# Four heads of the rotary self-attention are projected straight into the row tiles of the scores

## What is computed

```python
x = _layernorm(x + _L0_attn_ref(x, ...), axis=-1)
x = _layernorm(x + _L0_xattn_ref(x, ctx_1024, ...), axis=-1)
x = _layernorm(x + _L0_ffn_ref(x, ...), axis=-1)
x = _layernorm(x + _L1_attn_ref(x, L1_attn_Wq, L1_attn_bq, ...), axis=-1)
x = _layernorm(x + _L1_xattn_ref(x, ctx_1024, ...), axis=-1)
x = _layernorm(x + _L1_ffn_ref(x, ...), axis=-1)

def _L1_attn_ref(x, Wq, bq, Wk, bk, Wv, bv, Wo, bo):
    B, S, D, H = (4, 512, 256, 16)
...
    rx = _apply_rope(x)      # [x1 cos - x2 sin, x1 sin + x2 cos] over the two halves of the features

    def proj(W, bias):
        y = rx @ W.T + bias
        return y.reshape(b, s, h, hd).transpose(0, 2, 1, 3)
    q, k, v = (proj(Wq, bq), proj(Wk, bk), proj(Wv, bv))
    scores = jnp.einsum('bhqd,bhkd->bhqk', q, k) / np.sqrt(hd)
    attn = jax.nn.softmax(scores, axis=-1)
    attended = jnp.einsum('bhqk,bhkd->bhqd', attn, v)
    attended = attended.transpose(0, 2, 1, 3).reshape(b, s, d)
    return attended @ Wo.T + bo
```

## Time and profile before

| | us |
|---|---|
| median of 3 runs | 1947.82 |
| lowest and highest run | 1942.93, 1952.94 |
| the profiled execution | 1955.06 |
| its span in the profile | 1953.7 |
| `self_heads`, its first DMA | 560.7 |
| `self_heads`, first and last score matmul of L1566 | 612.8, 977.4 |

### The profile page before, as it was taken

One profiled execution on the slowest core, in us unless ns is written; L12 is line 12 of the kernel. 1 busy time (PEld: TensorE's weight loads), 2 busy tenths in 40 slices (PEclk: granted clock), 3 DMA queues, 4 the chain that ended last, 5 costly groups with the idle time before them and its releaser, 6 DMA issues. The chain is left out here.

```text
span 1953.7 us, 23728 instructions
## 1 busy us (share of the span) xinstructions
PE 1667.5 (85%) x7451; PEld 1216.7 (62%) x7451; DVE 1146.5 (59%) x2249; ACT 1012.8 (52%) x1936; POOL 985.7 (50%) x832
## 2 busy tenths in 40 slices
...
DMA packets 96930, 146.43 MB, mean 75 GB/s; under 512 B 22727, under 2 KB 61836, under 8 KB 93974
## 3 DMA queue, kind: packets, MB, share of 16 engines
...
## 5 line engine op out<-in xcount | busy, mean ns | idle before, releaser
L2414 POOL TENSOR_TENSOR STp_lo_use<-ST_use,STp_hi_use 128x512 fp32r<-128x512 f32 x256 | 338.0, 1330 | 197.2 <-ACT ST_use L2244 195.8
L1890 POOL TENSOR_TENSOR STp_lo<-ST,STp_hi 128x512 fp32r<-128x512 f32 x192 | 248.3, 1313 | 103.6 <-ACT ST L1651 102.3
L2309 DVE TENSOR_REDUCE nmax_use<-bank 128x1 f32<-128x512 f32 x256 | 173.4, 679 | 107.9 <-PE bank L2149 103.4
L2240 ACT ACTIVATE STp_hi_use<-bank 128x512 fp32r<-128x512 f32 x256 | 153.1, 598 | 158.8 <-PE bank L2175 154.8
L1777 DVE TENSOR_REDUCE nmax<-bank 128x1 f32<-128x512 f32 x256 | 170.8, 683 | 51.6 <-PE bank L1566 50.7
L1566 PE MATMUL bank<-rows_k,rows_q 65*128 65x512 f32 x256 | 134.5, 534 | 39.4 <-DVE nmax L1777 21.1
L2244 ACT ACTIVATE ST_use<-bank 128x512 f32<-128x512 f32 x256 | 151.7, 593 | 2.0 <-POOL STp_lo_use L2414 2.0
L1648 ACT ACTIVATE STp_hi<-bank 128x512 fp32r<-128x512 f32 x192 | 116.8, 608 | 57.7 <-PE bank L1577 57.3
L2149 PE MATMUL bank<-ks,qs 128*128 128x512 f32 x256 | 110.6, 433 | 9.4 <-DMA ks<-ks 8.8
L1651 ACT ACTIVATE ST<-bank 128x512 f32<-128x512 f32 x192 | 117.8, 614 | 0.0
...
L2159 PE MATMUL bank<-qs,ks 128*128 128x512 f32 x256 | 103.0, 402 | 7.2 <-DMA q<-rowbuf_use 7.1
...
...
## 6 DMA issues: line engine op xcount, KB each, us to landing
...
rows_q<-hop_scratch SPq DMA_DIRECT2D x32, 256.0 KB, 4.5
...
rows_k<-hop_scratch SPq DMA_DIRECT2D x24, 256.0 KB, 5.6
hop_scratch<-qkp_hi SPq DMA_DIRECT2D x20, 256.0 KB
...
```

The source lines that it names most:

```text
L1890: G.tensor_tensor(parts_of(u)[1], ST[u % TB], plain(parts_of(u)[0]), ALU.subtract).then_inc(low.sem, low.inc(u))
L2240: A.activation(STp[u % NHI][0], bk.ap, ACT.Exp)
L2309: V.tensor_reduce(nmax[:, (h % 2) * TB + j:(h % 2) * TB + j + 1], bk.ap, AX.X, ALU.max, negate=True).then_inc(bk.free, 1)
L2414: G.tensor_tensor(STp[u % NHI][1], ST[u % NFULL], plain(STp[u % NHI][0]), ALU.subtract).then_inc(low["pool"].sem, low["pool"].inc(u))
```

## The change

The first quarter of the first batch, heads 0 to 3, no longer takes the way through HBM. The host gives two more arrays: `first_W`, the columns of Wq and Wk of heads 0 to 3, each head's 16 columns twice, so 128 columns each; and `first_cols`, the biases in the same order and a column `odd` that is 1 on the second copy of each head. `first_heads` makes two projections of six matmuls with them, of q into one bank and of k into another. Each head then has 32 partitions there. ScalarE and VectorE write 32 partitions at a time into the rows of one head: ScalarE q high twice (`take_first`), VectorE q low twice and, through `odd`, k high and low in turn (`first_parts`), ScalarE a copy of these k rows into the next 32 partitions. Heads 0 and 1 are made ahead of step 0, heads 2 and 3 by VectorE at steps 3 and 6. The first score matmul of each of these heads waits for the parts of that head alone, and no longer for `stacked[0]`.

The general projections of the first batch move from steps -36 to -27 to the steps 0, 1, 4 and 5, V's from -24 to -18 to the steps 9 to 15, the placing of V to the steps 18, 21, ... 39. `average`, `root` and `norm` of the batches 1, 2 and 3 stand at the steps 8, 44 and 56 (`norm` two steps later). Hops of the first group in batch 0 leave out heads 0 to 3; SP issues all hops and row loads, those of quarter 1 at step 2, of quarters 2 and 3 at step 6.

All weights of the stage are loaded by SP, one behind the other, into tiles of their own that are not in use yet. ScalarE rounds Wq, Wk and Wv at the place -43, once all are there; GpSimd makes their low parts at -39. VectorE makes the first batch's four rotary products. The constant rows come by two DMAs from a small HBM tensor that the first stage writes, and GpSimd fills `Vone` at step 9.

```diff
-        stage = [turned[:, :, 0:D], part[:, :, 0:D]]
+        stage = [t.rearrange("p (c d) -> p c d", c=DC) for t in ST]
...
-        STACK = ((28, (0, 0), (0, 0)), (31, (1, 0), (0, 1)), (34, (0, 1), (1, 0)), (37, (1, 1), (1, 1)))
+        STACK = ((28, 0, (0, 0), (0, 0)), (31, 1, (1, 0), (0, 1)), (34, 4, (0, 1), (1, 0)), (37, 5, (1, 1), (1, 1)))
+        FIRST_MADE, NORMS = (-38, -37, 3, 6), (None, 8, 44, 56)
...
+            def first_heads(n):
+
+                bk = OUT_BANKS[n]
+                PE.wait_ge(bk.free, bk.use(("first", n), takers=HS))
+                PE.wait_ge(w_low.sem, w_low["first"])
+                for c in range(DC):
+                    PE.wait_ge(src_low.sem, src_low[0, c])
+                group(bk.ap, [(cut(first_W, slice(None), n, c), cut(srcp, slice(None), c)) for c in range(DC)]).then_inc(bk.full, 1)
...
+                if s == FIRST_MADE[0]:
+                    first_heads(0)
+                    first_heads(1)
                 if s == 0:
-                    PE.wait_ge(zeroed.sem, zeroed["rows"])
-                    PE.wait_ge(v_zeroed.sem, v_zeroed["V"])
+                    PE.wait_ge(zeroed.sem, zeroed["k"])
...
+                    if j == 0 and b == 0 and h < HS:
+                        for i in range(2):
+                            PE.wait_ge(OUT_BANKS[i].free, OUT_BANKS[i].free_at["first", i] - HS + 1 + h)
+                        PE.wait_ge(copied.sem, copied["copied", h])
+                    elif j == 0 and h % HS == 0:
...
+            A.wait_ge(staged[0].sem, staged[0]["cols"])
+            A.activation(first_W[0][:, 0], first_stage[:, 0], ACT.Copy, scale=scale["Wq1"])
+            A.activation(first_W[0][:, 1], first_stage[:, 1], ACT.Copy).then_inc(w_high.sem, w_high.inc("first"))
+            def take_first(h):
+                rows = slice(2 * h * HD, 2 * (h + 1) * HD)
+                A.wait_ge(OUT_BANKS[0].full, OUT_BANKS[0].full_at["first", 0])
+                A.activation(rows_q[0:2 * HD, h, :], OUT_BANKS[0].ap[rows], ACT.Identity, bias=first_bias[rows, 0:1], scale=1.0).then_inc(stack_high.sem, stack_high.inc(("first", h)))
...
+                if s == -43:
+                    A.wait_ge(staged[1].sem, staged[1]["bias"])
+                    A.activation(stage[0], stage[0], ACT.Copy, scale=scale["Wq1"]).then_inc(a_own.sem, a_own.inc("s4 Wq"))
+                    A.wait_ge(a_own.sem, a_own["s4 Wq"])
+                    for n, name in enumerate(names):
+                        A.activation(W[name][0], stage[n], ACT.Copy).then_inc(w_high.sem, w_high.inc(name))
...
+                    if s == FIRST_MADE[h] + 1:
+                        A.wait_ge(OUT_BANKS[1].free, OUT_BANKS[1].free_at["first", 1] - HS + 1 + h)
+                        A.activation(rows_k[2 * HD:4 * HD, h, :], plain(rows_k[0:2 * HD, h, :]), ACT.Copy).then_inc(copied.sem, copied.inc(("copied", h)))
+                if s == FIRST_MADE[0]:
+                    A.wait_ge(own.sem, own["s4 bias"])
+                    take_first(0)
+                    A.wait_ge(OUT_BANKS[1].full, OUT_BANKS[1].full_at["first", 1])
+                    A.activation(first_odd, OUT_BANKS[1].ap, ACT.Identity, bias=first_bias[:, 1:2], scale=odd).then_inc(stack_high.sem, stack_high.inc("odd"))
+                    take_first(1)
+                for h in range(2, HS):
+                    if s == -32 + h:
+                        take_first(h)
...
+                skip = HS if b == 0 and g == 0 else 0
+                engine.dma_start(hop_d[b % 2, n, g * H1 // 2 + skip:(g + 1) * H1 // 2, block * HD:(block + 1) * HD], plain(stack_out(b, n, p, g))[skip * HD:]).then_inc(hopped[n][g].sem, hopped[n][g].inc((b, k)))
...
+            def first_parts(h):
+
+                rows = slice(2 * h * HD, 2 * (h + 1) * HD)
+                V.wait_ge(stack_high.sem, stack_high["first", h])
+                V.scalar_tensor_tensor(rows_q[2 * HD:4 * HD, h, :], OUT_BANKS[0].ap[rows], first_bias[rows, 0:1], plain(rows_q[0:2 * HD, h, :]), ALU.add, ALU.subtract).then_inc(OUT_BANKS[0].free, 1)
+                V.wait_ge(stack_high.sem, stack_high["odd"])
+                V.scalar_tensor_tensor(rows_k[0:2 * HD, h, :], OUT_BANKS[1].ap[rows], first_cols[rows, 1:2], plain(first_odd[rows]), ALU.add, ALU.subtract).then_inc(OUT_BANKS[1].free, 1)
 
             average(0)
-            take_weights(0)
             norm(0)
-            take_weights(1)
-            take_weights(2)
-            V.wait_ge(kit.tables_in.sem, table)
+            V.wait_ge(w_high.sem, w_high["first"])
+            V.scalar_tensor_tensor(first_W[1][:, 0], first_stage[:, 0], scale["Wq1"], plain(first_W[0][:, 0]), ALU.mult, ALU.subtract)
+            V.tensor_tensor(first_W[1][:, 1], first_stage[:, 1], plain(first_W[0][:, 1]), ALU.subtract).then_inc(w_low.sem, w_low.inc("first"))
+            V.tensor_scalar(first_bias[:, 0:1], first_cols[:, 0:1], HD ** -0.5, None, ALU.mult)
+            V.tensor_tensor(first_bias[:, 1:2], first_cols[:, 1:2], odd, ALU.mult).then_inc(own.sem, own.inc("first bias"))
+            V.wait_ge(staged[1].sem, staged[1]["bias"])
...
+                if s == -43:
+                    for c in range(DC):
+                        V.wait_ge(turn_bank(0, c).free, turn_bank(0, c).free_at["x1", 0, c])
+                        for i in range(DC):
+                            m = V.tensor_tensor((turned, part)[c][:, i, :], xT[:, c, :], cs[:, i ^ c, :], ALU.mult)
+                    m.then_inc(own.sem, own.inc(("rope", 0, DC - 1)))
...
-                if of_next(s, 38) == 0:
-                    average(1)
-                    average(2)
-                    norm(1)
-                    average(3)
-                    norm(2)
-                    norm(3)
+                for k in range(1, B):
+                    if s == NORMS[k]:
+                        average(k)
+                    if s == NORMS[k] + 2:
+                        norm(k)
                 for t in range(TB):
-                    b = of_next(s, 40 + 2 * t)
-                    if b is not None:
-                        bk = v_bank(b, t)
+                    b = of_next(s, 40 + 2 * t, 9 + 2 * t)
...
-                    b = of_next(s, max(48 + g, (g + 1) * HG * TB + OUT_LAG))
+                    b = of_next(s, max(48 + g, (g + 1) * HG * TB + OUT_LAG), 18 + 3 * g)
...
+                if s == -39:
+                    G.wait_ge(src_low.sem, src_low[0, DC - 1])
+                    for n, name in enumerate(names):
+                        G.wait_ge(w_high.sem, w_high[name])
+                        G.tensor_tensor(W[name][1], stage[n], plain(W[name][0]), ALU.subtract).then_inc(w_low.sem, w_low.inc(name))
...
-                if of_next(s, 24) == 0:
-                    G.wait_ge(rope_part.sem, rope_part[0, DC - 1])
-                    G.memset(plain(rows_q[PARTS:ROWS]), 0.0).then_inc(g_own.sem, g_own.inc("s4 rows_q"))
-                    G.memset(plain(rows_k[PARTS:ROWS]), 1.0).then_inc(zeroed.sem, zeroed.inc("rows"))
-                    G.wait_ge(zeroed.sem, zeroed["rows"])
-                    G.wait_ge(own.sem, own["s4 V"])
+                for k in range(1, B):
+                    if s == NORMS[k]:
+                        root(k)
+                if s == NORMS[1] + 1:
+                    G.memset(plain(Vone), 0.0).then_inc(g_own.sem, g_own.inc("s4 V"))
+                    G.wait_ge(g_own.sem, g_own["s4 V"])
                     for g in range(GROUPS):
                         m = G.memset(plain(head_columns(g, ONE, 1)), 1.0)
                     m.then_inc(v_zeroed.sem, v_zeroed.inc("V"))
                     G.wait_ge(v_zeroed.sem, v_zeroed["V"])
-                if of_next(s, 38) == 0:
-                    root(1)
-                    root(2)
-                    root(3)
...
-            for n, name in enumerate(names):
-                if n > 1:
-                    SP.wait_ge(w_low.sem, w_low[names[n - 2]])
-                SP.dma_start(stage[n % 2], T[name]).then_inc(staged[n % 2].sem, staged[n % 2].inc(n // 2))
+            for name, dst, src in (("W", first_stage, T["first_W"]), ("cs", cs, T["cs"]), ("cols", first_cols, T["first_cols"])):
+                SP.dma_start(dst, src).then_inc(staged[0].sem, staged[0].inc(name))
+            for name, dst, src in (*((name, stage[n], T[name]) for n, name in enumerate(names)), ("bias", bqkv, T["bqkv"])):
+                SP.dma_start(dst, src).then_inc(staged[1].sem, staged[1].inc(name))
+            SP.wait_ge(kit.consts_in.sem, kit.consts_in["ones"])
+            for z, (rows, n) in enumerate(((rows_q, "q"), (rows_k, "k"))):
+                SP.dma_start(plain(rows[PARTS:ROWS]), bass.AP(kit.const_d.tensor, z * S, [[0, ROWS - PARTS], [0, H1], [1, S]])).then_inc(zeroed.sem, zeroed.inc(n))
             norm_loads(SP, (1, 2, 3))
...
-                    if of_next(s, 33 + 5 * g) == 0:
-                        SP.wait_ge(stack_bank(0, 0, g).free, stack_bank(0, 0, g).free_at["stack", 0, 0, g])
-                        hop(SP, 0, 0, g)
```

(6 more changed lines are left out.)

136 lines of the change are left out of this document (73 added, 63 removed).

## The result

| | before | after |
|---|---|---|
| median of 20 runs each | 1950.99 | 1955.63 |
| lowest and highest run | 1942.71, 1955.62 | 1949.73, 1965.12 |
| ratio, with its 95% interval | | 1.0034 (1.0021 to 1.0048) |
| the profiled execution's span | 1953.7 | 1962.9 |
| `self_heads`, its first DMA | 560.7 | 559.7 |

The change makes the kernel 0.34% slower, some 6.6 us by the ratio and 4.6 by the medians, where 12 us of gain were forecast. The first score comes 29.1 us earlier and the last 7.4 us later: 36.5 us go between the two. The profiled execution of the changed kernel, 1965.12 us, was the slowest of its 20, so its span is not held against another's; what follows compares times within the stage.

The account below looks back on a forecast made before the run. The bound was the fourth stage's start, 52 us to its first score, with TensorE waiting 18.3 us for a row DMA. Gain 17.1 - 2.0 - 2.0 - 1.0 = 12.1 us off median 1947.82: 1935.7, say 1936; 8 in 10, 1927 to 1947.

Parts of the forecast that it names:

- The start: Weight and bias loads, then VectorE's products: first matmul of the direct heads at 575.0 (573 to 578), against 584.7.
- the direct heads: Twelve matmuls, then ScalarE and VectorE parts in series, 7.5 us: first score at 582.5, 30.3 us before 612.8.
- Steps 0 to 16: VectorE's 20.1 us of work plus 6.0 of waits: step 16 at 608.6 against 625.67, gain 17.1 us.
- The fill of Vone: GpSimd's fill from step 9, first used at step 18: costs nothing, 2 us at most.
- The statistics and normalisation of batches 3 and 4: At steps 44 and 56, blocks of 1.8 and 1.4 us, partly covered by score banks: together 2.0 us (0.5 to 6).
- V and rotary work in steps 17 to 45: V placements on VectorE, some 0.5 us a pair: three beside rope cost 1.5 us, three more 0.5.
- The row of maxima: 8 KB row queued behind 2.0 MB of row loads, needed for the first transposed scores: costs 1.0 us (0 to 4).
- Given back later: Half clock and longer waits through step 16, statistics costing 6: gain 4, 1944; within 0.30 shared with late cases.
- Late rows: Second quarter's rows, needed at step 16, come 1.8 us late: gain 7, 1941; within a shared 0.30.
- Slower: the clock: TensorE at 1.2 GHz from step 28 through 64, 1.0 us more a step: 24 us above forecast, 1960; chance 0.08.

Follow-up runs that it names:

- e3_act_norm: The changed kernel with the normalisations of batches 2 to 4 made by ScalarE at the same steps, not VectorE: ratio 0.9975 to the kernel before, median 1945.5.
- e1_fill_early: The changed kernel with GpSimd's fill of Vone right behind the low parts of the weights, not at step 9: ratio 1.0007 to the kernel before, median 1952.1.
- e6_before_norms_late: The kernel before with only statistics, roots and normalisations of batches 2 to 4 moved to steps 8, 44 and 56: ratio 1.0102, median 1972.2.
- e5_accum: The changed kernel with VectorE's three normalisations also writing an accumulator, a measurement with wrong values: ratio 0.9976 to the kernel before, median 1945.4.
- e2_norms_ahead: The changed kernel with statistics, roots and normalisations of batches 2 to 4 back ahead of step 0: ratio 1.0022 to the kernel before, median 1954.4.

## Why the prediction was wrong, point by point

The forecast was a gain of 12.1 us, and the stage lost 8.3: they are 20.4 us apart. By the prediction's own terms, 8.1 of it lie in steps 0 to 16, 2.7 in V and rotary work up to step 45, 7.1 in the statistics and normalisations of steps 45 to 64, and 3.8 in the last 15 steps, for which it had no term; 0.3 and the 1.0 of the row of maxima came back. The step that failed is the price of VectorE's normalisations: 1.4 us each, taken from a stretch where GpSimd was idle. At their new places, beside GpSimd's work, they took 8.04, 2.75 and 5.19 us, and where TensorE waited behind them its granted clock fell.

- **The start** and **the direct heads** were right. First matmul of the direct heads 576.64 (573 to 578 forecast), with the bias 1.7 us later than forecast (571.2) and the stage 1.0 us earlier; first score 583.69 against 582.5. From the first matmul to the score 7.05 us, forecast 7.5. The operations on 32 partitions took 0.74 to 0.76 us on VectorE and 0.63 on ScalarE, as those on 128, so pricing them alike was right. GpSimd's low parts of weights took 1.27 each and were hidden.
- **Steps 0 to 16** was wrong as it stands: step 16 gained 9.0 us, forecast 17.1. The sum itself was sound: with the normalisation off VectorE (e3_act_norm) the gain is 16.5, with it at 1.38 us (e1_fill_early) 13.4, and 2.5 us of what is missing there went in steps 0 to 8 at the lower clock. (Its parts as listed add up to 19.8 and not 20.1, which changes nothing.) What it had wrong is one term, "statistics of the second batch 1.8 and its normalisation 1.4": 8.04 us, not 1.4.
- **The fill of Vone**, "nothing, and 2 at most", is that same error from the other side. I asked who needs the fill and by when, and never whom it stands beside. It costs 6.7 us (8.04 less 1.38 in e1_fill_early; 7.5 at the stage's end).
- **The statistics and normalisation of batches 3 and 4**, "2.0 (0.5 to 6)", is the mis-sized term that decides: 9.1 us in steps 45 to 64, 11.1 when done alone (e6_before_norms_late). Counting TensorE's longer busy time as the clock and the rest as waits, the 9.1 are 3.6 of clock and 5.5 of waits, and the 11.1 are 5.3 and 5.8. With tiles that are never held (e5_accum) the same steps take 4.4 more than before, 1.5 of clock and 2.9 of waits. The forecast's 2.0 knew only waits of tiles that are never held, and against 2.9 it is not far off; the hold adds 2.6 us of waits, and for the clock the term had nothing. The granted clock was 1.00 there before and 0.81 to 0.94 in every kernel with late blocks, so it is no cause of its own: in e2_norms_ahead, without such blocks, it was 0.93 and the steps took 25.0 us against 24.1. I took 1.4 us from the earlier trace rows, where GpSimd is idle, and moved it to where it is busy 17.34 of 20; I saw that busy share and used it only for GpSimd's delay. The trace of before had the answer, in the pipeline itself: the source view of the finished batches' normalisation.

```profile
L1873 DVE TENSOR_SCALAR X<-summed,mv,rstd x12: 396/405/1396, 774.0 to 961.9; 128x256 f32<-128x256 f32 x12
```

- **V and rotary work in steps 17 to 45** was put at 2.0 and came with the rest of those steps to 4.7 (3.1 in e1_fill_early, 6.3 in e3_act_norm). The placements were priced at 0.5 us a pair from the earlier trace rows, again beside an idle GpSimd; in steps 16 to 45 eight pairs took 9.98 us and not 4.1, with casts and subtractions that last as long as the low part beside them. That is 5.9 us more of VectorE's time, the same mistake as with the normalisations; the trace of before had it too, with casts of 215 to 1319 ns. How much of it reached the end of the stage, beside the products and the clock (0.76 against 0.79), no run tells apart.
- **The row of maxima**, 1.0 (0 to 4), cost nothing in the changed kernel, because VectorE was later. Once VectorE was relieved the wait was there, 4.9 and 7.9 us. By the rule of the Trainium skill, DMA: Bandwidth & Descriptors (Queues, rings and completion order), that each DMA engine takes the descriptors of one ring in order, I had weighed it at 1 to 3; the traces agree with the rule, and the price was higher.
- **The rivals.** *Given back later* has the direction and one of the causes, but sized at 6 what measured 9.1. *Late rows* did not happen: the last row loads of quarter 2 were issued by 599.7 and landed within 4.0 us, and step 16 waited for VectorE. The doubt behind it was sound, though: while the half hops ran alone, from 590 to 595, the DMA share was 0.25 at 80 GB/s, against 0.5 and up to 195 for whole hops in the earlier trace rows. *Slower: the clock* named the right engine and the wrong form, and its sum is wrong too: 36 steps at 1.0 us each are 36 us off the forecast, 1972, and not 24 and 1960. The clock did not stay low from step 28 on; it fell for some microseconds behind a hole (0.83 on average from 690 to 710), and once more at the stage's end: 3.8 us in the last 15 steps that I had not forecast.
- **The range** (1927 to 1947) had no room for this: several terms were bounded by durations from stretches with GpSimd idle, so they were low together.
